# A graph attention stage in which SyncE fetches one of four groups of 128 rows of every 20th batch, one load a row, in place of a gather

## What is computed

```python
h = jnp.maximum(_layernorm(x, axis=-1), 0.0)
h_prime = (h @ W + b).reshape(n, K, F_OUT)              # 6250 x 8 heads x 32
h_src = jnp.sum(h_prime * a_src, axis=2)
h_trg = jnp.sum(h_prime * a_trg, axis=2)
e = leaky_relu(h_src[src] + h_trg[trg], 0.2)
exp_e = jnp.exp(e - jnp.max(e))
denom = segment_sum(exp_e, trg)
msg = h_prime[src] * (exp_e / (denom[trg] + 1e-10))[:, :, None]
x = x + segment_sum(msg, trg).reshape(n, 256)
```

## Time and profile before

| | |
|---|---|
| median of 3 runs | 3159.29 us (3156.21 to 3159.81) |
| profiled execution, span | 3157.3 us |
| the runs' median less the span | 2.0 us |
| first and last gather of the attention stage | 2114.6 and 3103.3 us |
| busy share of the span: PE, DVE, POOL, ACT | 77%, 68%, 63%, 47% |

### The profile page before, as it was taken

The page is one execution under the profiler, slowest core; times in us unless marked ns, Lnnn a source line. Parts: engine busy times, 40 slices in busy tenths (PEclk is TensorE's granted clock), DMA queues, the critical chain, the costliest instruction groups (busy, mean ns, idle before and its releaser), DMA issues. The chain is left out here.

```text
span 3157.3 us, 79016 instructions
## 1 busy us (share of the span) xinstructions
PE 2446.9 (77%) x25310; PEld 2164.9 (69%) x25311; DVE 2156.6 (68%) x3833; ACT 1488.6 (47%) x3803; POOL 1976.9 (63%) x2143
## 2 busy tenths in 40 slices
PE   0577777777777789999999999947777777777763
PEld 0466666666666679999999999945555555555552
DVE  7676667777677636666666666657766766666666
ACT  5444444444444458888888888831111111111114
POOL 4677777777777634444444444437777777777772
PEclk9998889999899889999999999978888888887996
DMA  6555555555555500000000000026555655555554
GB/s 158 168 161 149 158 154 166 161 163 160 159 164 158 143 25 18 21 21 20 20 21 20 20 22 21 21 61 178 171 173 173 174 172 168 173 172 173 171 170 136
DMA packets 183839, 373.69 MB, mean 118 GB/s; under 512 B 42598, under 2 KB 93688, under 8 KB 183769
## 3 DMA queue, kind: packets, MB, share of 16 engines
q0 software_dynamic: 75552, 209.66, 23.5%
q1 hardware_dynamic: 107392, 162.37, 17.4%
q10 hardware_dynamic: 824, 0.87, 0.1%
HBM read 346.95 MB, written 25.80 MB: 118 GB/s over the span
## 5 line engine op out<-in xcount | busy, mean ns | idle before, releaser
L446 POOL DMA_INDIRECT rows<-tab_scratch,srcs x784 | 765.7, 977 | 238.7 <-issue 234.1
L1458 POOL DMA_INDIRECT a_rows<-tab_scratch,srcs x784 | 750.5, 957 | 251.7 <-issue 235.8
L1524 PE MATMUL sum_ps<-feat,a_hot 128*125 128x264 f32 x1960 | 601.5, 463 | 237.5 <-DVE feat L1616 121.0
L1524 PEld LDWEIGHTS sum_ps<-feat,a_hot 128*125 128x125 f32 x1960 | 417.4, 222 | 341.7 <-DVE feat L1616 133.9
L876 PE MATMUL z_ps<-ah,w 128*128 128x125 f16 x6400 | 553.8, 219 | 1.0 <-PEq L982 1.0
L876 PE MATMUL z_ps<-al,w 128*128 128x125 f16 x3200 | 542.7, 217 | 0.0
L876 PEld LDWEIGHTS z_ps<-ah,w 128*128 128x128 f16 x6400 | 489.5, 97 | 1.5 <-issue 1.4
L1468 ACT ACTIVATE feat<-d 128x32 f32<-128x32 f32 x196 | 44.9, 229 | 827.0 <-DVE d L1612 566.2
L500 PE MATMUL mlp_ps<-ewa,eab 128*128 128x256 f16 x788 | 203.5, 290 | 284.3 <-PEq L496 283.3
L478 ACT ACTIVATE rh<-mlp_ps 128x1024 f16<-128x1024 f32 x196 | 199.7, 1019 | 358.2 <-ACTq L477 347.7
L829 POOL TENSOR_TENSOR a<-a 128x500 f32<-128x500 f32 x100 | 124.4, 1244 | 372.1 <-POOLq L828 372.1
(11 more groups left out here) (211 smaller groups left out, 5422.8 us busy)
## 6 DMA issues: line engine op xcount, KB each, us to landing
ea<-edge_t SPq DMA_DIRECT2D x394, 128.0 KB
dstb<-dst_flat SPq DMA_DIRECT2D x98, 512.0 KB
rows<-tab_scratch,srcs POOLq DMA_INDIRECT x784
a_rows<-tab_scratch,srcs POOLq DMA_INDIRECT x784
tab_scratch<-prow SPq DMA_DIRECT2D x50, 128.9 KB
hx<-x SPq DMA_DIRECT2D x50, 125.0 KB
x_scratch<-x SPq DMA_DIRECT2D x50, 125.0 KB
hs<-tab_scratch SPq DMA_DIRECT2D x50, 125.0 KB
```

Of the source, the lines that this page charges most:

```text
L446: pool.indirect_dma_start(rows[:, b % DEEP, k, :], None, dram["tab0"], bass.IndirectOffsetOnAxis(ap=srcs[:, c:c + 1], axis=0),).then_inc(r ...
L1458: pool.indirect_dma_start(rows[:, b % DEEP, k, :], None, dram["tab1"], bass.IndirectOffsetOnAxis(ap=srcs[:, c:c + 1], axis=0),).then_inc(r ...
L1524: ins = pe.matmul(out[:], hot[:, h, k, :], feat[:, row, k, :], start=(k == 0), stop=(k == CB - 1))
```

## The change

For 9 of the 196 batches (b = 19, 39, ..., 179, APART = 20) POOL issues three gathers, not four. The 128 rows of the fourth group are loaded by SP, one DMA of 1056 bytes a row, into a tile beside the ring (`side`, two halves). SP does so in the 18 batches ahead: in each turn it issues 7 or 8 of these loads (128 in 18 turns), *before* it waits for the gathers of that batch. The row's number is data, so SP first loads up to four numbers from a tile in SBUF (`side_at`) into registers, then works out an address for each and issues the DMA. In the 20th turn SP waits for all 128 rows, copies `side` to its group of the ring with one DMA, waits until that has landed, and goes on as before. The wait for the gathers now counts three of them in these batches.

```diff
+        APART = 20
+        GROUPS = NB // APART
+        side = m.sb("a_side", [P, 2, TW], F32)
+        side_at = m.sb("a_side_at", [1, GROUPS, P], I32)
...
+            at_end = APART * BE - P
+            sp.dma_start(side_at[:], t["src_flat"].rearrange("(g e) -> g e", e=APART * BE)[0:GROUPS, at_end:at_end + P].unsqueeze(0)).then_inc(ld_side_at, 16)
+
+            def side_rows(g, first, last):
+                for r in range(first, last, 4):
+                    n = min(4, last - r)
+                    _, nodes_ = nc.values_load_multi_w_load_instructions(
+                        side_at[0:1, g, r:r + n], engines=[mybir.EngineType.SP], min_val=0, max_val=N - 1,
+                        skip_runtime_bounds_check_because="src numbers the nodes, 0 to N - 1")
+                    for j, v in enumerate(nodes_):
+                        sp.dma_start(side[r + j:r + j + 1, g % 2, :], dram["tab1"][bass.ds(v, 1), :]).then_inc(side_in[g % 2], 16)
+
             load_self(NT - 1)
             load_x1(slice(LAST + 1, NT))
+            sp.wait_ge(ld_side_at, 16)
+            STEPS = APART - 2
+
+            def landed(b):
+                return sum(CB - (at % APART == APART - 1) for at in range(b % DEEP, b + 1, DEEP))
+
             for b in range(NB):
                 i, u = divmod(b, RING)
-                sp.wait_ge(rows_ready[b % DEEP], 16 * CB * (b // DEEP + 1))
+                g, turn = divmod(b, APART)
+                if g < GROUPS and turn < STEPS:
+                    side_rows(g, turn * P // STEPS, (turn + 1) * P // STEPS)
+                if g < GROUPS and turn == APART - 1:
+                    sp.wait_ge(side_in[g % 2], 16 * P)
+                    sp.sem_inc(side_in[g % 2], -16 * P)
+                    sp.wait_ge(rows_free, b - DEEP + 1)
+                    sp.dma_start(rows[:, b % DEEP, CB - 1, :], side[:, g % 2, :]).then_inc(side_kept, 16)
+                    sp.wait_ge(side_kept, 16 * (g + 1))
+                sp.wait_ge(rows_ready[b % DEEP], 16 * landed(b))
                 sp.sem_inc(rows_in, 1)
...
-                for k in range(CB):
+                for k in range(CB - 1 if b % APART == APART - 1 else CB):
...
+    a["src_flat"] = src
```

More of the change, by code:

```diff
@@ L1363, in edges1 @@
         ld_x1 = m.sem("ld_x1")
+        ld_side_at = m.sem("ld_side_at")
+        side_kept = m.sem("side_kept")
+        side_in = [m.sem(f"side_in{h}") for h in range(2)]
         smax_in, smax_turned = m.sem("smax_in"), m.sem("smax_turned")
```

## The result

The changed kernel takes 3287.26 us (3286.83 to 3294.34, 4 runs) against 3159.55 (3156.21 to 3160.64, 4 runs) of the kernel before. The ratio is 1.0409, 95% interval 1.0394 to 1.0424: 128 us slower, where 98 were forecast. 3287 lies inside the range of 3190 to 3320.

What follows compares the result with a forecast made beforehand. POOL's gather issue bounds the attention stage before, SP after: 22.6 + 89.1 = 111.7 us per 20 batches against 100.9. Nine groups at 10.8 us over add 97.5, giving a median of 3257 us, range 3190 to 3320.

Steps and rivals of the forecast that it cites:

- What bounds the kernel: Attention stage: POOL's gather issue sets the pace before, 100.9 us per 20 batches; SP becomes the bound after, 111.7 us.
- What is removed: Nine gathers at 1.261 us leave POOL: 11.3 us, the whole result if POOL stayed the bound.
- The row loads: SP's address, move and DMA for each side row: 0.455 us a row, 58.2 us a group of 128.
- The register loads: SP's 36 loads of row numbers a group: 28.1 us, cheaper for four numbers from a multiple of four.
- The copy: SP's copy of the side tile to the ring, issue and wait: 2.8 us a group.
- one of its own signs: Sign in SP's trace: the forecast is wrong if a register load of four takes less than 0.5 us.
- The sum: SP's side work: 89.1 us a group against 78.3 of slack, 10.8 too much; SP's own need 22.6.
- What stands behind it: After SP's late signal: u = 2 some 8 us after u = 1; POOL's 35 us lead only delays its waiting.
- The end: Last 16 batches, without side rows: give-back of up to 9 us set against unevenly used SP slack, at nothing.
- POOL as the bound: Rival: register loads cost as one access, 12.4 us a group, so SP's work fits; 3148 us, chance 0.08.
- A fixed price a load: Rival: SP loads up to four registers in 0.551 us, side work 82.1 us; +34 us, 3194, chance 0.13.
- DMAs that cost more: Rival: 0.545 us a row on SP, a group 11.5 us dearer; +201 us, 3360, chance 0.09.

Runs made afterwards that it cites:

- experiment 1: Changed kernel without the nine side groups: no row loads, no copies, POOL's nine gathers also gone; 3147.99 us, ratio 0.9965 to the kernel before.
- experiment 2: Changed kernel with SP's row loads kept, but POOL gathering all four groups and nothing copied; 3272.66 us, ratio 1.0361 to the kernel before.
- experiment 3: Changed kernel without the nine copies and the waits for them; POOL still issues nine gathers fewer; 3273.96 us, ratio 1.0362 to the kernel before.
- experiment 4: Changed kernel fetching rows of fixed numbers, without register loads, address instructions and moves; 3150.91 us, ratio 0.9976 to the kernel before.
- experiment 5: Changed kernel with 16 turns of 8 rows, so every register load begins at a multiple of four; 3221.80 us, ratio 1.0196 to the kernel before.
- experiment 7: Changed kernel with one register load of sixteen numbers every second turn, rows still ahead of the signal; 3184.59 us, ratio 1.0078 to the kernel before.
- experiment 6: Changed kernel with the row loads issued after the batch's signal and before the wait for hs_free; 3183.71 us, ratio 1.0079 to the kernel before.
- experiment 8: Changed kernel with sixteen numbers a register load and the rows after the signal; 3150.78 us, ratio 0.9973 to the kernel before.
- experiment 9: Sixteen-number loads and rows after the signal, but every 16th batch, twelve groups, one half of the side tile; 3144.24 us, ratio 0.9959 to the kernel before.
- experiment 10: Changed kernel with all register loads but a quarter of the rows, POOL gathering all groups, nothing copied; 3158.61 us, ratio 1.0003 to the kernel before.

## Why the prediction came out as it did

**What bounds the kernel.** Right: POOL before (experiment 1), SP after. The mechanism held, and the forecast came out 30 us low because terms of the sum were off, some of them in opposite directions.

**What is removed.** 11.3 us forecast, 10.8 measured in experiment 1; in the changed kernel the nine gathers are worth nothing (experiments 2 and 3).

**The row loads.** 58.2 us a group forecast, 55 measured: 37 + 29 + 228 ns and three gaps for most rows (three in four), some 40 ns more for the first row after each register load, and 1.1 us a group of single longer gaps. This timeline row of SP (2391.4 to 2392.4 us; start, duration) holds three loads in one line, so from first to third start they take (1.05 - 0.23) / 2 = 0.41 us each:

```profile
2391.46 1.05 SPq L1450 DMA_DIRECT2D a_side<-tab_scratch  x3
```

The DMA of one row takes 228 ns and not the 263 that I took, save for the first after a register load (0.27, as in the last row of the timeline further down). The page counts 187054 packets against 183839, 3215 more and not the 1152 that I named; experiment 4 has 187034 of them and loses nothing.

**The register loads.** This is the term that was sized too low: 28.1 us forecast, 33.6 measured: 8 x 0.51 + 12 x 1.11 + 16 x 0.94 = 32.4 us by the means of the three kinds, and 1.2 us of gaps. Four loads of turns with 7 rows, at four places, show the three prices: four numbers from a multiple of four, three numbers, four from elsewhere, and again four from elsewhere:

```profile
L1446 SPq TENSOR_LOAD <-a_side_at x1: 498/498/498, 2390.4 to 2390.4; - x1
...
L1446 SPq TENSOR_LOAD <-a_side_at x1: 949/949/949, 2392.6 to 2392.6; - x1
...
L1446 SPq TENSOR_LOAD <-a_side_at x1: 1058/1058/1058, 2394.9 to 2394.9; - x1
...
L1446 SPq TENSOR_LOAD <-a_side_at x1: 1140/1140/1140, 2403.2 to 2403.2; - x1
```

I had 0.31, 0.77 and 1.00: each load costs SP some 0.1 to 0.2 us more than DVE and PE. The shape was right, that four from a multiple of four are much cheaper: experiment 5 halves the loss by it, and sixteen cost 1.2 us. That such four cost as one isn't shown, since SP loads no single number. By one of its own signs the forecast would be wrong: it allowed no load of four under 0.5 us, and the 72 that begin at a multiple of four have a median of 0.49. The sign contradicted the sum, which had put these very loads at 0.31. That SP pays more than DVE for a load couldn't be read before, since SP had none. The Trainium skill's figure (Runtime: NRT & Kernel Launch, Instruction fetch mechanics) of some 200 ns a register holds for none of these as it stands: three numbers cost 310 ns each, four from a multiple of four 125, four from elsewhere some 275, sixteen 75.

**The copy.** 2.8 us forecast, 4.1 for the wait and 0.5 for the issue measured, 1.8 us a group too little. In effect it is 13 us over nine groups (experiment 3), under what it takes.

**The sum.** SP's records account for its whole time. The table gives us in 20 batches, as the mean of the eight stretches from SP's signal for batch 19 to that for batch 179; each part has the short gaps behind its instructions in it, and a pause of more than 0.12 us counts as a wait where SP waits for another's signal or a landing.

| kernel | rows | register loads | copy | waits for DVE | SP's other work | waits for gathers | together |
|---|---|---|---|---|---|---|---|
| before | 0 | 0 | 0 | 12.9 | 9.3 | 78.8 | 101.0 |
| changed | 55.3 | 33.6 | 4.6 | 12.1 | 10.3 | 0.1 | 116.0 |
| experiment 3, no copy | 55.1 | 33.6 | 0 | 15.3 | 10.2 | 0.1 | 114.3 |
| experiment 5, eight rows a turn | 55.0 | 18.5 | 4.4 | 20.9 | 10.3 | 0 | 109.1 |
| experiment 7, sixteen numbers | 54.3 | 9.9 | 4.7 | 25.6 | 10.3 | 0 | 104.8 |
| experiment 6, after the signal | 55.2 | 33.0 | 4.6 | 0.6 | 10.6 | 0 | 104.0 |
| experiment 8, both | 54.0 | 9.4 | 4.4 | 4.5 | 10.4 | 17.3 | 100.0 |

Side work is 93.5 us a group, against 89.1 forecast, and SP's own need 22.4, against 22.6. With 0.1 for gathers that makes the 116.0 measured, where the forecast had 111.7. Of the 4.3 us missing, the register loads are 5.5 and the copy 1.8; the rows were put 2.9 too high, which hid a part of it.

The table shows a second thing, which the forecast had no term for. Ahead of the signal, what SP saves comes back in part as waits for DVE: experiment 7 saves 23.7 us of register loads and wins 11.2 us of pace, since the waits grow from 12.1 to 25.6. Behind the signal (experiment 6) the waits shrink to 0.6, and with the whole side work in place the pace is 104.0.

**What stands behind it.** The adding up at u = 1 came as told: where the turn has rows, the signal of u = 2 comes 8.3 us after that of u = 1 in the mean (forecast some 8). DVE's idle time before `e` put down to SP rose by 126 us (forecast about 100). POOL's idle time for DVE is 171.7 us and not 70 to 90, or some 136 beyond the usual 0.3 us before each of these 118 gathers, and it begins at 2242 us, at the end of the first group and not after the third. So POOL's lead was used up much sooner than the 35 us that I gave it; why wasn't followed. One such place in the timeline (2399.8 to 2404.6 us): `dstb` right after the signal, DVE's `hs`, SP's load of `hs`, POOL kept waiting by DVE, and the first row load of the next turn:

```profile
2399.95 0.37 SPq L1424 DMA_DIRECT2D dstb<-dst_flat  x1
...
2402.47 0.42 DVE L1661 TENSOR_TENSOR acc<-acc,hs 125x256 f32 x1
...
2402.91 0.27 SPq L1438 DMA_DIRECT2D hs<-tab_scratch  x1
...
2404.42 0.94 POOL L1492 DMA_INDIRECT a_rows<-tab_scratch,srcs  x1 [1.26 <-DVE a_hot L1666]
2404.53 0.27 SPq L1450 DMA_DIRECT2D a_side<-tab_scratch  x1
```

Here 4.6 us go by after the signal before a row is issued, 2.6 of them in the wait for `hs_free` and 1.1 in the register load. Experiment 6 shows what the place of the rows is worth: 104 us. The prediction saw the mechanism but counted the wait only as a part of SP's need.

**The end.** I set the give-back of the last 16 batches (up to 9 us) against uneven slack at nothing. Counted from DVE's first `e` to its last, the stage takes 1104.0 us, against 975.8 before: 128.2 more, as much as the medians differ by. Up to batch 19 it loses 22.2 us (107.9 against 85.7; at its start the kernel before still runs at 4.5 us a batch), in the eight groups after that 120.1 us (927.8 against 807.7), and in the last 16 batches 14.1 us come back (68.3 against 82.4). So the nine groups cost 142 us and not 97.5, and the give-back of 14 us hides a part of that. That the forecast is only 30 us low and lies inside its range owes something to luck: the rows that were put too high (26 us in nine groups) and this give-back stand against the terms that were put too low. The profiled execution is 7 us above the median, and its attention stage starts 7 us later than that of before, for which nothing in the change is a reason.

**The rivals.** POOL as the bound: right as a mechanism (experiments 4, 8, 9), but the condition that I gave it was too kind. In experiment 7 the register loads take 9.9 us a group, below 12.4, and the kernel still takes 3185 us and not 3148, since the rows stand ahead of the signal. A fixed price a load: wrong (0.49 to 1.14). DMAs that cost more: wrong, they cost less; the longest of the 1152 took 283 ns, and nothing like the 1.46 us each of the earlier trace rows shows.

## What to carry to other kernels

An engine that waits most of the time isn't free. Sum what it must do itself and what it waits for from engines that wait for it in turn; the rest is its slack. A job beyond the slack costs time (93 us of work in 78 of slack cost 128 us in the end), and one far below it cost nothing here (48 us). Near the threshold the place decides as well: in front of the signal, 69 us of work in 77 of slack still cost 25 us. Put such a job behind the signal and ahead of the next wait, where its time falls into a wait that is there anyway; that alone was worth 104 us. Load register values in few, long, aligned instructions, before counting the DMAs that they address.

## What wasn't expected of the hardware

- TensorE's granted clock fell although it had less to do. The windows from 2200 to 3000 us of before and from 2200 to 3100 of after (length, then busy time and count by engine, PE's granted clock, DMA share, GB/s) give 0.85 and 0.78 of full speed, while PE is busy for 75% and 71% of the time:

```profile
2200.00:3000.00 800.00, 601.44 (x4288) 454.83 (x4287) 553.59 (x1310) 121.40 (x635) 606.84 (x635) 0.85 0.59 172
```

```profile
2200.00:3100.00 900.00, 635.59 (x4210) 477.68 (x4209) 541.90 (x1283) 119.17 (x622) 589.09 (x621) 0.78 0.53 152
```

  The two levels are 1.2 and 2.4 GHz, so a larger part of the stretch was at the lower one, and the sums' matmuls (L1558, L1524 before) took 508 ns in the mean from 2150 to 3100 us (462 before). The other kernels go much the same way from 2200 to 3000 us: 0.79 and 0.77 in experiments 2 and 3 (PE busy for 71%), 0.81 in experiment 5 (72%), 0.83 in experiments 6 and 7 (74%), and 0.85 or 0.86 in experiments 1, 4, 8, 9 and 10 (75% or 76%). Up to the last copy it goes with the loss and doesn't make it: SP's waits for DVE, through which a slower PE would reach SP, are 12.1 us in 20 batches, against 12.9 before the change.
- The price of a register load depends on where it starts, by a factor of two for four numbers (0.49 and 1.06 to 1.14 us on SP).
- In the changed kernel SP waits 56.3 us in 21 waits for `hs_free` from 2150 to 2650 us (2.7 each), and 48.5 us in 23 from 2650 to 3175 us (2.1 each), with the same instructions. The starts of the copies follow each other at 119 us first and at 114 to 115 us in the end. What shrinks is the time from the signal of u = 1 to the start of DVE's `e`, from 1.4 us in the mean to 0.8; in the first part `e` waits for PE's `a_used_ps` in most of these rounds. It shrinks before the change too (1.4 to 1.1), so the change isn't its reason. The cause stays open.
